# Expert layers of a six-layer kernel in tiles of 128 slots, with the tokens stationary and the weights moving

## The reference

```python
# C: 16 experts of width 256, 4 for each token, and one shared expert
h = silu(einsum('td,eid->tei', xf, w1)) * einsum('td,eid->tei', xf, w3)
y = einsum('tei,edi,te->td', h, w2, comb)         # comb: zero except for the 4 chosen experts
z = silu(xf @ ws1.T) * (xf @ ws3.T) @ ws2.T       # shared expert, every token
# F: 8 experts of width 1024, 2 for each token, no shared expert, softmax weights
hidden = silu(h1) * h2 ; y = sum(total_probs * (hidden @ w3.T))
```

## Time and profile before

| | |
|---|---|
| runs | 2470.38, 2476.36, 2479.93 us; median 2476.36 |
| span of the profiled execution | 2457.6 us, 37707 instructions |
| outside the span, against the median | 18.8 us |
| PE busy | 2120.9 us, 86% of the span |
| DVE, ACT, POOL busy | 1130.6, 897.9, 950.9 us |
| moved by DMA | 299 MB, mean 122 GB/s |
| expert stage C, first to last matmul | 573.4 to 904.6 us |
| expert stage F, first to last matmul | 1894.9 to 2421.2 us |

### The profile page before, as it was taken

How to read it: one execution, slowest core, us unless ns; L and a number is a source line. 1 busy time by engine, 2 the same in 40 slices (tenths; PEclk the granted TensorE clock), 3 DMA queues, 4 the chain that set the end, 5 groups by cost and what they waited for, 6 DMA issues and landing times. The chain is left out here.

```text
span 2457.6 us, 37707 instructions
## 1 busy us (share of the span) xinstructions
PE 2120.9 (86%) x13252; PEld 1820.9 (74%) x13252; DVE 1130.6 (46%) x2057; ACT 897.9 (37%) x1479; POOL 950.9 (39%) x641
## 2 busy tenths in 40 slices
PE   6895888837999975999999999986765999999994
PEld 5543766637999963788888888865544999999993
DVE  4145463765555565232233222348664445544542
ACT  2112121215666642223232323223222555555551
POOL 2002312005777773232223222213212666666654
PEclk9996999958999987999999999968886999999997
DMA  3483000016888883011001100010003566656653
GB/s 124 169 313 115 18 23 29 1 35 245 274 283 276 282 277 128 18 30 33 26 26 28 33 26 26 18 48 5 22 6 142 200 217 213 209 199 219 214 192 124
DMA packets 102450, 298.99 MB, mean 122 GB/s; under 512 B 10912, under 2 KB 27936, under 8 KB 102336
## 3 DMA queue, kind: packets, MB, share of 16 engines
q1 hardware_dynamic: 76928, 232.88, 28.3%
q0 software_dynamic: 11840, 38.81, 5.2%
q10 hardware_dynamic: 13600, 26.22, 2.8%
HBM read 265.10 MB, written 32.77 MB: 121 GB/s over the span
## 5 line engine op out<-in xcount | busy, mean ns | idle before, releaser
L134 PE MATMUL banks<-ra 128*128 128x256 f32 (+3 forms) x3004 | 982.9, 327 | 55.9 <-DVE x L1040 24.7
L135 PE MATMUL banks<-ra 128*128 128x256 f32 (+3 forms) x3004 | 967.4, 322 | 0.0
L136 PE MATMUL banks<-ra 128*128 128x256 f32 (+3 forms) x3004 | 964.0, 321 | 0.0
L134 PEld LDWEIGHTS banks<-ra 128*128 128x128 f32 (+1 forms) x3004 | 577.9, 193 | 119.5 <-issue 39.5
L136 PEld LDWEIGHTS banks<-ra 128*128 128x128 f32 (+1 forms) x3004 | 577.7, 192 | 43.7
L135 PEld LDWEIGHTS banks<-ra 128*128 128x128 f32 (+1 forms) x3004 | 579.4, 193 | 36.1
L1475 POOL TENSOR_TENSOR ra<-fa,ra 128x1024 fp32r<-128x1024 f32 x187 | 445.9, 2385 | 235.3 <-ACT ra L1508 234.4
L1508 ACT ACTIVATE ra<-fa 128x1536 fp32r<-128x1536 f32 x190 | 281.5, 1482 | 85.1 <-DMA fa<-in_L_units 67.9
L1592 DVE TENSOR_TENSOR ra<-fa,ra 128x256 fp32r<-128x256 f32 x190 | 162.7, 856 | 92.0 <-ACT ra L1532 92.0
L332 POOL TENSOR_TENSOR ra<-fa,ra 128x2048 fp32r<-128x2048 f32 (+2 forms) x22 | 85.7, 3905 | 284.3 <-ACT ra L326 277.4
L1567 DVE TENSOR_TENSOR ra<-fa,ra 128x512 fp32r<-128x512 f32 x190 | 133.6, 703 | 114.9 <-ACT ra L1508 108.2
(11 more groups left out here) (222 smaller groups left out, 2608.4 us busy)
## 6 DMA issues: line engine op xcount, KB each, us to landing
fa<-in_L_units SPq DMA_DIRECT2D x190, 768.0 KB, 4.3
fa<-in_ctxT SPq DMA_DIRECT2D x64, 514.0 KB, 5.3
ea_y_scratch<-fa ACTq DMA_DIRECT2D x35, 512.0 KB, 4.5
fa<-in_ctx SPq DMA_DIRECT2D x32, 512.0 KB, 5.3
eb_y_scratch<-fa ACTq DMA_DIRECT2D x15, 512.0 KB, 3.7
fa<-in_L_attn_w_qkvT SPq DMA_DIRECT2D x6, 1024.0 KB, 6.2
normed_scratch<-na SPq DMA_DIRECT2D x16, 256.0 KB, 2.1
x<-in_x SPq DMA_DIRECT2D x1, 2048.0 KB, 8.2
```

The lines of the kernel that those rows point to most:

```text
L134: pe.matmul(psum, lh, rh, start=first, stop=False)
L135: pe.matmul(psum, lh, rl, start=False, stop=False)
L136: return pe.matmul(psum, ll, rh, start=False, stop=last)
```

## The change

CAP becomes 128. There are then 47 + 8 tiles in C and 23 in F, hence 110 and 184 units, each with the same 768 KB of weights. A tile has one indirect gather, four transposes, one bank of y, of 256 KB. In `up` the tokens (128x128) are stationary and the weights move: one matmul covers both up blocks (2 x 128 columns) for one of four chunks, so `up` is 12 matmuls of 256 columns. The result has tokens on partitions; silu and the product run on 128 columns, h is turned by one PE transpose (`turn_h`) between the first two and the last two chunks of `up(n + 1)`, and DVE makes its high part and then its low part from PSUM. ACT no longer makes the high part of h. `down` is 3 matmuls of 512 columns. ACT now takes `rows_high` before `keep_y`. The low parts of the weights are split evenly, 768 columns on POOL and 768 on DVE (before 1024 and 512). In C the adds that go beside PE's work cover 4 units instead of 2.

```diff
-CAP = 2 * P
+CAP = P
...
+            HB, YB, XB, TB = 0, 2, 4, 6
+            POOLED = 3 * D // 2
...
-                        for s in range(2):
-                            pool.indirect_dma_start(xt[u][:, s, :], None, normed_dram, bass.IndirectOffsetOnAxis(
-                                ap=ids[u].bitcast(U32)[:, s:s + 1], axis=0)).then_inc(s_rows[u], 16)
+                        pool.indirect_dma_start(xt[u], None, normed_dram, bass.IndirectOffsetOnAxis(
+                            ap=ids[u].bitcast(U32), axis=0)).then_inc(s_rows[u], 16)
...
-                        pool.tensor_tensor(wl[b][:, 0:2, :], st[b][:, 0:2, :], wh[b][:, 0:2, :].bitcast(F32),
+                        own = slice(0, POOLED)
+                        pool.tensor_tensor(wl[b][:, own], st[b][:, own], wh[b][:, own].bitcast(F32),
                                            ALU.subtract).then_inc(s_wp, 1)
...
                     def hidden(n, b):
                         eng.wait_ge(s_h, n + 1)
+
+                        eng.wait_ge(s_hf, n + 1)
                         act.activation(sg[b], banks[:, HB + b, 0:CAP], ACT.Silu).then_inc(s_sg, 1)
-                        eng.wait_ge(s_hf, n + 1 + LEAD)
-
-                        eng.wait_ge(s_y, n + (W - 1))
-                        act.activation(hh_[b], hf[b], ACT.Copy).then_inc(s_hh, 1)
...
                             hidden(n, q % 2)
+                            if q == TURN and there(j + 1, TILES):
+                                rows_high(j + 1, 1 - u)
                             if q == 0 and not (isinstance(j, int) and j == 0):
                                 keep_y(j, u, i)
-                            if q == TURN and there(j + 1, TILES):
-                                rows_high(j + 1, 1 - u)
...
-                        dve.tensor_tensor(wl[b][:, 2, :], st[b][:, 2, :], wh[b][:, 2, :].bitcast(F32),
+                        own = slice(POOLED, 3 * D)
+                        dve.tensor_tensor(wl[b][:, own], st[b][:, own], wh[b][:, own].bitcast(F32),
                                           ALU.subtract).then_inc(s_wd, 1)
...
                             eng.wait_ge(s_sg, n + 1)
+
+                            eng.wait_ge(s_ht, n + 1)
                             dve.tensor_tensor(hf[b], banks[:, HB + b, CAP:2 * CAP], sg[b], ALU.mult).then_inc(s_hf, 1)
-                            eng.wait_ge(s_hh, n + 1)
-                            dve.tensor_tensor(hl[b], hf[b], hh_[b].bitcast(F32), ALU.subtract).then_inc(s_hl, 1)
                             if q == TURN and there(j + 1, TILES):
                                 rows_low(j + 1, 1 - u)
+
+                            eng.wait_ge(s_ht, n + 1 + LEAD)
+                            eng.wait_ge(s_y, n + (W - 1))
+                            dve.tensor_copy(hh_[b], banks[:, TB + b, 0:CAP]).then_inc(s_hh, 1)
+                            eng.wait_ge(s_hh, n + 1)
+                            dve.tensor_tensor(hl[b], banks[:, TB + b, 0:CAP], hh_[b].bitcast(F32),
+                                              ALU.subtract).then_inc(s_hl, 1)
...
-                            if plan.shared and isinstance(j, int) and j == TILES - 1:
-                                add_rows(eng, range(q * QUARTER, (q + 1) * QUARTER))
+                            if plan.shared and isinstance(j, int) and j >= TILES - 2:
+                                part = U * (j - TILES + 2) + q
+                                add_rows(eng, range(part * QUARTER, (part + 1) * QUARTER))
...
+                        for c in which:
+                            ins = mm3(banks[:, HB + q % 2, 0:2 * CAP], gh[u][:, c, :], gl[u][:, c, :], up_part(wh[b], c),
+                                      up_part(wl[b], c), c == 0, c == DC - 1)
...
+                    def turn_h(n, q):
+                        eng.wait_ge(s_hf, n + 1 + LEAD)
 
                         eng.wait_ge(s_hl, n + 1)
...
+                        pe.transpose(banks[:, TB + q % 2, 0:CAP], hf[q % 2], ident[:]).then_inc(s_ht, 1)
+
+                    def down(n, j, u, q, b):
+
+                        eng.wait_ge(s_hl, n + 1 + LEAD)
...
+                            if following:
+                                up(*following, FIRST)
+                            turn_h(n, q)
+                            if following:
+                                up(*following, REST)
+                            down(n, j, u, q, (U * u + q) % W)
+
+                    FIRST, REST = range(0, 2), range(2, DC)
```

More of the change, by code:

```diff
@@ L1133, in __init__ @@
                 self.weight = f.take(self.kinds, NT)
-                self.token = f.take(2 * self.tiles)
+                self.columns = self.tiles + self.tiles % 2
+                self.token = f.take(self.columns)
                 self.expert = f.take(self.tiles)
@@ L1139, in routing @@
             layer, E, K = plan.layer, plan.experts, plan.choices
-            KN, H = plan.kinds * NT, 2 * plan.tiles
+            KN, H = plan.kinds * NT, plan.columns
             f = Area(fa, F_SIZE, plan.at)
@@ L1352, in experts @@
             s_stored = [sem(f"{tag}_stored{u}") for u in range(2)]
[L1353 to L1356, removed]
+            (s_wh, s_wp, s_wd, s_h, s_sg, s_hf, s_ht, s_hh, s_hl, s_y, s_kept, s_ids, s_passed, s_turned, s_xh, s_xl) = (
+                sem(f"{tag}_{n}") for n in ("w_high", "w_low_pool", "w_low_vector", "h_products", "silu", "h", "h_turned",
+                                            "h_high", "h_low", "y", "y_kept", "ids", "passed", "turned", "x_high",
+                                            "x_low"))
+            HB, YB, XB, TB = 0, 2, 4, 6
+            POOLED = 3 * D // 2
             PEELED = 3
@@ L1571, in rows_low @@
                         eng.wait_ge(s_xh, j + 1)
[L1572 to L1576, removed]
+                        dve.tensor_tensor(gl[u], chunks(banks[:, XB, :]), gh[u].bitcast(F32),
+                                          ALU.subtract).then_inc(s_xl, 1)
                     eng.sem_inc(s_wd, W)
                     eng.sem_inc(s_hf, LEAD)
+                    eng.sem_inc(s_hl, LEAD)
                     eng.sem_inc(s_xl, 1)
@@ L1608, in _ @@
                     eng.sem_inc(s_turned, LEAD)
+                    eng.sem_inc(s_ht, LEAD)
                     def turn(j, u, i):
-                        eng.wait_ge(s_rows[u], 32 * i + 32)
+                        eng.wait_ge(s_rows[u], 16 * i + 16)
                         eng.wait_ge(s_xl, j + 1)
[L1615 to L1618, removed]
+                        for c in range(DC):
+                            cols = slice(c * P, (c + 1) * P)
+                            ins = pe.transpose(banks[:, XB, cols], xt[u][:, cols], ident[:])
@@ L1635, in down, with up @@
-                    def down(n, j, q, b):
-                        eng.wait_ge(s_hl, n + 1)
[L1638 to L1645, removed]
+                    def up(n, j, u, q, b, which):
+                        if 0 in which:
+                            if q == 0:
+                                eng.wait_ge(s_xl, j + 2)
+                            eng.wait_ge(s_wp, n + 1 + W)
+                            eng.wait_ge(s_wd, n + 1 + W)
+                            eng.wait_ge(s_hf, n + 1)
+                        for c in which:
+                            ins = mm3(banks[:, HB + q % 2, 0:2 * CAP], gh[u][:, c, :], gl[u][:, c, :], up_part(wh[b], c),
+                                      up_part(wl[b], c), c == 0, c == DC - 1)
+                        if DC - 1 in which:
+                            ins.then_inc(s_h, 1)
@@ new lines, in turn_h @@
+                    def turn_h(n, q):
+                        eng.wait_ge(s_hf, n + 1 + LEAD)
+                        eng.wait_ge(s_hl, n + 1)
+                        pe.transpose(banks[:, TB + q % 2, 0:CAP], hf[q % 2], ident[:]).then_inc(s_ht, 1)
+                    def down(n, j, u, q, b):
+                        eng.wait_ge(s_hl, n + 1 + LEAD)
+                        if q == 0 and not (isinstance(j, int) and j == 0):
+                            eng.wait_ge(s_kept, j)
+                        ins = mm3(banks[:, YB + u, :], hh_[q % 2], hl[q % 2], wh[b][:, 2 * D:3 * D], wl[b][:, 2 * D:3 * D],
+                                  q == 0, q == U - 1)
@@ L1653, in tile @@
                             if q < U - 1:
-                                up(n + 1, j, u, q + 1, (U * u + q + 1) % W)
+                                following = (n + 1, j, u, q + 1, (U * u + q + 1) % W)
                             elif there(j + 1, TILES):
-                                up(n + 1, j + 1, 1 - u, 0, (U * u + q + 1) % W)
-                            down(n, j, q, (U * u + q) % W)
+                                following = (n + 1, j + 1, 1 - u, 0, (U * u + q + 1) % W)
+                            else:
+                                following = None
+                            if following:
[5 more added lines that the diff above has]
+                    FIRST, REST = range(0, 2), range(2, DC)
```

(2 more changed lines are left out.)

35 lines of the change are left out of this document (12 added, 23 removed).

## The result

The changed kernel takes 2690.19 us (median of 4 runs, 2687.82 to 2724.05) against 2473.37 for the kernel before on the same occasions: ratio 1.0914, 95% interval 1.086 to 1.0967. The forecast was 2491, its range 2410 to 2555. The direction was right and the size was not: some 217 us came where 15 were forecast.

What follows compares the result with a forecast made beforehand. PE bounded C and F before; after the change, chains of waits between engines would. C +49, F -30 and stage starts -4 made +15 us, which on 2476.4 gave 2491, range 2410 to 2555.

Steps and rivals of the forecast that it cites:

- the lock between DVE and POOL: Their subtractions of SBUF operands exclude each other: 2.30 us a unit, just under the 2.46 of F; costed at nothing.
- Rival (d): POOL takes the lock first and DVE's product waits; in one unit of four +55 us, 2546; chance 0.07.
- The chains: Waits from engine to engine set the pace: tile of C 6.92 us (+49 in all), of F 21.6 (-30).
- The 18.8 us: Whole kernel: the runs' median lies 18.8 us above the profiled span, so the forecast was put on 2476.4.
- `keep_y`: On ACT in the first unit of a tile, with its store: 1.25 us in C's chain, +1.0 in F's.
- Rival (b): PE and DMA bound, not the chains: F at 420 us, C at 352, in all 2387; chance 0.28.
- Rival (c): PE's gaps cost granted clock, with C busy 70 to 80%; chance 0.12.
- a clock below 0.95 in C: Sign in the profile after, PE's granted clock in stage C, listed among those that would show the prediction wrong.
- none of C's gaps is above 1.5 us: Argument against lost clock: PE's gaps in stage C stay at or below 1.5 us.
- Rival (e): Transfers fall behind at a 96% share: +25 us, 2516; chance 0.08.
- the DMA engines, forecast above 0.9: Sign in the profile after: DMA share above 0.9, with transfers hidden by the chains.

Runs made afterwards that it cites:

- e1: Changed kernel with DVE's low part of the weights reading its second operand from a bank of zeros in PSUM, so without the lock: 2492.06 us.
- e10: Changed kernel with 10 (C) and 14 (F) unused floats ahead of the work area that holds the staged weights: 2508.55 us.
- e13: Changed kernel with 16 unused floats ahead of the work area that holds the staged weights: 2680.65 us.
- e14: Changed kernel with 2 unused floats ahead of the work area that holds the staged weights: 2512.49 us.
- e7: Changed kernel with POOL's low part waiting for DVE's of the same unit, and 512 columns on POOL, 1024 on DVE: 2530.78 us.
- e9: e7 with keep_y and its store behind the high part of the weights on ACT: 2491.28 us, ratio 1.0081 to the kernel before.
- e6: Changed kernel with keep_y and its store behind the high part of the weights on ACT: 2609.64 us.
- e5: Changed kernel where weight loads after the first four of each layer bring 64 columns instead of 1536: 2694.52 us.
- e15: Kernel before with 6 and 2 unused floats, so staged weights begin at 192 and 80 floats: 2472.28 us.
- e12: e9 with the unused floats of e10 ahead of the work area: 2465.99 us.
- e3: Changed kernel with 512 columns of the low parts on POOL and 1024 on DVE: 2580.59 us.
- e4: Changed kernel with 1024 columns of the low parts on POOL and 512 on DVE: 2786.33 us.

## Why the prediction was wrong

**The step that failed** is the lock between DVE and POOL: "I cost it at nothing in the sum; the cover is thin." Its measured cost is 198 us (e1). Two things in it were mis-sized. POOL's 768 columns were priced at 1.54 us from the rows of before; they took 1.79 at best and 1.85 in the mean where POOL never waited (e1), since the work area had moved from 186 and 78 floats to 192 and 80 (e10, e13 and e14 show it). The lock was thus wanted for 0.76 + 1.85 = 2.61 us of a unit of 2.46, not for 2.30. This term alone is worth 168 us (e13 against e14). And I took a wait for the lock as one POOL instruction long at most; with a backlog POOL made three low parts before DVE was served, 19 times in F. Behind such waits PE also ran at a granted clock of 0.50: 79 of the 205 us in the two stages are slower matmuls.

**Rival (d)**, POOL first, is what happened, and it had 0.07 of the chances. Its price, 55 us for one unit in four, was too low for the same two reasons and left out the clock.

**The chains came out about right**, as e1 shows without the lock: a tile of C took 6.9 to 7.0 us (6.92), one of F 21.95 (21.6). From first to last matmul of weights e1's C took 391.5 us (380 forecast) and F 508.2 (497), each some 11 us over. That the whole came to 2492.06 against a forecast of 2491 is partly luck. Over the kernel before, e1's span is 33 us longer where 15 had been forecast, and its time 19 us longer beside the same kernel. The 18.8 us that were put on top of the span do not exist: the later runs have 1.7 to 1.8 us outside of their own spans, so the profiled execution of before was about 2459 us (an estimate) and faster than the three timed ones. `keep_y` was priced at 1.25 us in a tile of C and gave 0.81 (e7 to e9). In F it was priced at 1.0 and gave 0.3 in e6 and nothing in e9.

**Rival (b)**, no chain, is refuted for C by e1: 391.5 us where it had 352. **Rival (c)**, clock lost to gaps: the gaps of the chain, 0.8 to 0.9 us, cost nothing (1.00 in C with PE 81% busy, e1). But its sign, a clock below 0.95 in C, did come true in the changed kernel, at 0.90, with waits of 1.83 us that the lock made. Against (c) stood "none of C's gaps is above 1.5 us", which holds only without the lock; that shorter gaps cost no clock was an estimate of mine, for which no row spoke (of the 25 waits of 1.52 to 1.57 us in C of e6, 2 were followed by 0.50). **Rival (e)**, transfers, is refuted by e5 for the changed kernel; the DMA engines, forecast above 0.9, were at 0.75 there and at 0.89 in C without the lock.

**Who is served next** is not told by the order of asking alone. In the ordinary unit it is: POOL at 2208.55, DVE at 2209.02, and DVE waits 1.27 us. But at 2198.36 DVE asked before POOL's second and third low part and was served behind both, after 5.30 us. The counts above (51 of 51 and 43 of 46) stood neither in my working nor in the rows that I read.

Left open: why POOL keeps the lock when its running instruction has not waited, and why its subtraction is slower with the staged operand at some places. Places 2, 10 and 14 floats past a multiple of 16 floats were fast (e14, e10), multiples of 16 slow (changed, e13, e15). A place 4 or 8 floats past was not tried, so the step that counts can be smaller than 64 bytes, nor was it tried which of the three operands matters.

## What to carry to other kernels

When an instruction pair shares an exclusive resource, add up both holders over the new, shorter period, with the price of each at the slow end, and treat a sum near the period as a loss: the one that loses the race delays everything behind it in its own program order (here the product, the transpose and PE's clock). Halving PE's time per unit is worth little where other engines keep their work per unit. A time that comes out as forecast proves no term: the 1.30 us of e6 were about half clock. And before a split of work is tuned, shift the buffers by a few bytes: here that was worth more than any one order or split.

## What the runs showed of the hardware

- POOL's subtraction (two SBUF inputs, float32 to fp32r) takes 1.09, 1.54 and 2.01 us at the shortest for 512, 768 and 1024 columns where the staged operand begins 202 and 94 (e12 and e10) or 186 and 78 floats (before) from the start of its tensor, in C and F; 1.54 for 768 at 194 and 82 too (e14). At 192 and 80 floats it takes 1.26 to 1.28, 1.79 and 2.33 (e7 and e3, changed, e4), and 1.79 for 768 at 208 and 96 (e13). DVE's instruction of 768 columns takes 0.94 to 0.95 at the shortest at 192 and 80 (changed) as at 202 and 94 (e10).
- A DVE subtraction of two SBUF operands that starts while POOL runs one low part and has the next ready (changed): served next in 51 cases of 51 where POOL's running one had itself waited, passed in 43 of 46 where it had not. The longest were 5.6 us in the changed kernel and 7.0 in e4.
- POOL's copy of 128x1 took 0.91 us in the median of 78 where DVE's subtraction had two SBUF operands (changed), and 0.18 to 0.20 in all 78 cases where DVE's second operand was in PSUM (e1).
- With its second operand in PSUM DVE's instruction of 768 columns takes 0.94 to 0.96 us in all 294 cases, and POOL's of 768 columns 1.80 to 1.88 beside it: neither waits for the other (e1).
- Of 24 waits of PE of 1.82 to 1.85 us in C of the changed kernel, 23 were followed by a stretch at a granted clock of 0.50; of 25 waits of 1.52 to 1.57 us in C of e6, two were, while a wait of 1.92 there was not. So the length of one wait does not decide it alone.
